# A preact-conv pair on one core: five written-out programs, a shorter first-unit program for GpSimd, and the last residual in the sums

## What is computed

```python
    def _L1_conv_ref(x, w1, w3, w5, wd, wf):
        ...
        x1 = _conv(x, w1, padding=[(0, 0), (0, 0)])
        x2 = _conv(x, w3, padding=[(1, 1), (1, 1)])
        x3 = _conv(x, w5, padding=[(2, 2), (2, 2)])
        x4 = _conv(x, wd, padding=[(2, 2), (2, 2)], dilation=(2, 2))
        out = jnp.concatenate([x1, x2, x3, x4], axis=1)
        return _conv(out, wf, padding=[(0, 0), (0, 0)])
    ...
    x = x + _L0_conv_ref(_gn(x), ...)
    x = x + _L1_conv_ref(_gn(x), w1, w3, w5, wd, wf)
```

## Time and profile before

| | us |
|---|---|
| median of 3 runs | 1725.4 (1724.74 to 1725.86) |
| the profiled execution | 1725.26 |
| its span, first to last instruction | 1723.0 |
| PE busy | 1645.8 (96% of the span) |
| DVE busy | 1492.8 (87%) |
| ACT busy | 1011.6 (59%) |
| GpSimd (POOL) busy | 637.2 (37%) |

### The profile page before, as it was taken

The page is one execution under the profiler, slowest core; times in us unless marked ns, Lnnn a source line. Parts: engine busy times, 40 slices in busy tenths (PEclk is TensorE's granted clock), DMA queues, the critical chain, the costliest instruction groups (busy, mean ns, idle before and its releaser), DMA issues.

```text
span 1723.0 us, 39391 instructions
## 1 busy us (share of the span) xinstructions
PE 1645.8 (96%) x13285; PEld 1550.5 (90%) x13285; DVE 1492.8 (87%) x1930; ACT 1011.6 (59%) x1647; POOL 637.2 (37%) x446
## 2 busy tenths in 40 slices
PE   6999989999999997999999999899999999899998
PEld 5989959999999994999999996799999999599998
DVE  6798879999788859999978886999987887799996
ACT  2866667455285657645546666655447565765541
POOL 5799962222381005232247003323227400512232
PEclk9999979999999998999999998899999999799999
DMA  7012115666502201566630220366651121055553
GB/s 190 0 42 61 45 31 126 169 165 171 148 19 57 72 19 39 149 168 177 165 99 14 73 60 1 86 164 174 168 159 46 41 69 38 1 137 132 140 146 95
DMA packets 101181, 166.05 MB, mean 96 GB/s; under 512 B 40010, under 2 KB 74411, under 8 KB 100940
## 3 DMA queue, kind: packets, MB, share of 16 engines
q1 hardware_dynamic: 77932, 138.95, 31.8%
q10 hardware_dynamic: 23168, 26.04, 4.8%
HBM read 52.20 MB, written 25.17 MB: 45 GB/s over the span
## 4 chain that ended last, share of the span: by engine, by line
PE 70%; DVE 12%; issue 11%; ACT 3%; POOL 1%; SPq 1%; DMA 1%; DVEq 1%; ACTq 0%; POOLq 0%
PE ps L924 28%; PE ps L772 12%; PE ps L793 8%; PE ps L795 7%; PE ps L794 7%; PE ps L821 3%; PE ps L855 3%; DVE region L1557 1%; DVE region L1587 1%; DVE region L1508 1%; POOL region L670 1%; PE ps L735 1%; DVE region L1605 1%; PE ps L919 1%; DMA region<-region 1%
## 5 line engine op out<-in xcount | busy, mean ns | idle before, releaser
L924 PE MATMUL ps<-region,W 128*96 128x256 f16 (+4 forms) x7156 | 796.7, 270 | 5.7 <-DMA region<-region 5.7
L924 PEld LDWEIGHTS ps<-region,W 128*96 128x96 f16 (+2 forms) x7156 | 774.9, 122 | 20.6 <-issue 14.1
L1346 DVE TENSOR_TENSOR region<-V,band 128x2322 f32<-128x2322 f32 (+2 forms) x104 | 257.7, 2488 | 59.2 <-PE ps L795 56.1
L1122 ACT ACTIVATE region<-region 96x1584 f16<-96x1584 f32 (+1 forms) x80 | 98.1, 1273 | 311.0 <-DVE region L1519 306.2
L680 POOL TENSOR_TENSOR region<-region 96x528 f32<-96x528 f32 (+1 forms) x72 | 96.4, 1344 | 407.8 <-DVE region L1557 405.8
L793 PE MATMUL ps<-region 128*128 (+1 forms) x1152 | 228.2, 280 | 10.0 <-DVE region L1355 4.4
L795 PE MATMUL ps<-region 128*128 (+1 forms) x1152 | 222.8, 275 | 0.0
L794 PE MATMUL ps<-region 128*128 (+1 forms) x1152 | 222.3, 275 | 0.0
L1587 DVE SCALAR_TENSOR_TENSOR region<-ps,small,region 96x768 f32<-96x768 f32 (+1 forms) x220 | 203.7, 988 | 10.3 <-PE ps L924 8.5
L772 PE MATMUL ps<-proj,region 96*128 96x240 f32 x1024 | 210.1, 368 | 0.5 <-DVE region L1605 0.4
L772 PEld LDWEIGHTS ps<-proj,region 96*128 96x128 f32 x1024 | 195.2, 191 | 14.4 <-issue 1.2
(11 more groups left out here) (208 smaller groups left out, 2229.6 us busy)
## 6 DMA issues: line engine op xcount, KB each, us to landing
region<-region SPq DMA_DIRECT2D x116, 247.5 KB, 4.0
region<-in_x_dram SPq DMA_DIRECT2D x128, 192.0 KB, 2.4
out_dram<-region SPq DMA_DIRECT2D x40, 576.0 KB, 4.2
region<-region ACTq DMA_DIRECT2D x72, 247.5 KB, 2.4
X<-in_x_dram SPq DMA_DIRECT2D x30, 576.0 KB, 5.9
region<-region SPq DMA_DIRECT2D x36, 247.4 KB, 4.9
X<-in_x_dram SPq DMA_DIRECT2D x19, 384.0 KB, 11.1
region<-region SPq DMA_DIRECT2D x24, 185.6 KB, 3.8
```

Of the source, the lines that this page charges most:

```text
L924: last = mm(o, w, src, start=k == 0, stop=k == len(steps) - 1, skip_group_check=split and ck > 0)
L1346: v.tensor_tensor(T[:, i, 3 * c:3 * c + m].rearrange("p m (i j) -> p m i j", j=3), taps.broadcast_to([P, m, BW // 3, 3]), mask.broadcast_t ...
```

## The change

1. The loops over the images in SP's, GpSimd's and ACT's programs become Python loops: the four images are written out, semaphore values are constants, and the branches on `b` go.
2. GpSimd's `first_planes` ends after the differences and part 0 of blocks 1 to 4. Part 1's points and its column sums, for all five blocks, move to DVE (`second_part_edge`, `second_part`), in between the low parts of part 0 and those of part 1. They are now made by two multiply-adds and one addition.
3. The mean is put back by ACT (one activation with bias `MG2`, twice the mean, for which DVE has a new tiny step) instead of DVE.
4. ACT's order in the first unit: the copies of part 0 go ahead of part 1's high parts.
5. Last unit: DVE adds `X` to two of the three kinds of sums in `acc`, ahead of `middle_outputs`; GpSimd's `residual` for it goes, and SP's write waits for DVE.

```diff
@@ first_planes (GpSimd)
-                    twice = f32at(Y2F_AT + YF * RW, 5 * RW).rearrange("p (k e) -> p k e", k=5)
+                    twice = f32at(Y2F_AT + YF * RW, 4 * RW).rearrange("p (k e) -> p k e", k=4)
-                    def point_0_and_inf(k, end, n):
-                        done(n)
-                        take(twice[:, k:end], plane(k, end, 1), plane(k, end, 0))
-                        take(plane(k, end, 2), plane(k, end, 2), plane(k, end, 1))
-                        done(n + 2)
-                        take(plane(k, end, 0), twice[:, k:end], plane(k, end, 0))
-                        take(plane(k, end, 2), plane(k, end, 2), plane(k, end, 1))
-                        done(n + 4)
...
                     for c in range(2):
                         take(slots(0, 3, c), taps(2, c, 3), taps(0, c, 3))
-                    point_0_and_inf(1, 5, 13)
-                    column_sums(1, 5, 0, 3)
-                    pool.wait_ge(s_pl0, b * NPL0 + 1 + START)
-                    own = yb.rearrange("p r e -> p (r e)")
-                    take(pln[:, 0, 0:3 * RW], own[:, 2 * RW:], own[:, 0:3 * RW])
-                    point_0_and_inf(0, 1, 19)
-                    column_sums(0, 1, 0, 3)
...
-                for u in range(UNITS - 3, UNITS):
-                    residual(u, LASTR if u == UNITS - 1 else UR)
+                for u in range(UNITS - 3, UNITS - 1):
+                    residual(u, UR)
@@ ACT
+                one = buffers(0)[2][:, 1:5, 4 * RW:5 * RW].rearrange("p k (c j) -> p k c j", c=2)[:, :, :, 1:1 + HC]
+                act.wait_ge(s_fp, b * NFP + 10 + START)
+                act.wait_ge(s_st, sv + N_MEAN2 + 2 + START)
+                act.activation(one, one, ACT.Identity, bias=col(MG2)).then_inc(s_fix, 1)
                 deviation(N_PPRE + b * NPST + 7, 7, 1)
...
-                        act.wait_ge(s_fp, b * NFP + 23 + START)
+                        copied(0, 2)
+                        act.wait_ge(s_pl0, b * NPL0 + 8 + START)
                         plain(hi, 1)
-                        copied(0, 2)
-                        act.wait_ge(s_fp, b * NFP + 24 + START)
+                        act.wait_ge(s_pl0, b * NPL0 + 9 + START)
                         sums(hi, 1)
@@ DVE
+                def second_part_edge():
+
+                    own = yb.rearrange("p r e -> p (r e)")
+                    v.tensor_tensor(plane0(0, 0, 3), own[:, 2 * RW:], own[:, 0:3 * RW], ALU.subtract).then_inc(s_pl0, 1)
+
+                def second_part():
+
+                    slot = lambda k: pln0[:, :, k * RW:(k + 1) * RW]
+                    first_done(6)
+                    dve.wait_ge(s_fp, b * NFP + 13 + START)
+                    v.scalar_tensor_tensor(slot(0), slot(0), -2.0, slot(1), ALU.mult, ALU.add).then_inc(s_pl0, 1)
+                    v.scalar_tensor_tensor(slot(2), slot(1), -2.0, slot(2), ALU.mult, ALU.add).then_inc(s_pl0, 1)
+                    first_done(8)
+                    pairs = pln0[:, :, 0:3 * RW].rearrange("p k (q e) -> p k q e", e=RW)
+                    v.tensor_tensor(cs0[1].rearrange("p k (q j) -> p k q j", j=PC), pairs[:, :, :, PC:RW],
+                                    pairs[:, :, :, 1:1 + PC], ALU.add).then_inc(s_pl0, 1)
...
-                for part in range(2):
-                    lows(0, 0, 0, 0, part)
+                second_part_edge()
+                lows(0, 0, 0, 0, 0)
+                second_part()
+                lows(0, 0, 0, 0, 1)
...
                 first_rows(UNITS - 1, 2, LASTB)
+                dve.wait_ge(s_acc, (b * UNITS + UNITS - 1) * NACC + 5 + START)
+                rows = X[:, (UNITS - 1) * UR * W:].rearrange("p (r j c) -> p c r j", j=HC, c=2)
+                for r in range(OR):
+                    n = len(range(r, LASTR, OR))
+                    kinds = acc[:, r, 1:3, 0:n * HC].rearrange("p c (k j) -> p c k j", j=HC)
+                    v.tensor_tensor(kinds, kinds, rows[:, :, r:LASTR:OR], ALU.add).then_inc(s_pre, 1)
+                dve.wait_ge(s_pre, (b + 1) * OR + START)
                 middle_outputs(UNITS - 1, LASTB)
```

61 lines of the change are left out of this document (31 added, 30 removed).

## The result

The changed kernel takes **1711.99 us** (median of 4 runs, 1711.63 to 1713.19) against 1725.12 us for the kernel before, measured beside it (1724.74 to 1725.86). The ratio is 0.9925, 95% interval 0.9907 to 0.9942: faster by 13.1 us, 10 to 16. The forecast was 1717.2 with a range of 1711.5 to 1725.5; the time lies in the range, near its lower end.

The account below looks back on a forecast made before the run. The prediction held each image to hang on when unit 1's low parts are placed. First unit 6.5 plus last unit 1.7 gave 8.2 us off 1725.26, 1717.1; adjusted for the median it predicted 1717.2, range 1711.5 to 1725.5.

Parts of the forecast that it names:

- GpSimd stops earlier, 4.1 us per image: x1's statistics on DVE: tiny steps no longer held by GpSimd, variance 4.1 us earlier, 3.4 in the second image.
- The mean on ACT, 0: First unit: ACT's activation of about 0.75 us is hidden before the root is wanted, so it costs nothing.
- Part 1 on DVE takes back 2.3 us: First unit, counted from S (end of L1488): L1511 starts at S+11.3, was S+8.97, losing 2.3 us per image.
- I count nothing for them: The first unit's last low DMAs, which must land ahead of L1557: issued 1.1 or 1.7 us earlier, priced at zero.
- One for one through unit 1's low parts: Every microsecond by which DVE reaches the end of L1557 earlier is a microsecond of the image.
- Net of the first unit 6.5 us: First unit over four images: 1.8 us gained in each of three images and 1.1 in the second.
- The last unit 1.7 us, and nothing between images: DVE's additions replace GpSimd's residual: 1.7 us gained at the program's end, nothing between images.
- Loops written out, "I count zero": ACT's 2.60 us stop at the loop's return: removal worth zero; on the path, three would give 7.8 us.
- This rival: PE's clock drops in the longer wait at unit 1: 2.6 us an image, 1727.6 if all fall; chance 0.12.
- The rival that the hold isn't GpSimd's: DVE's tiny steps stay at 1.24 us, so nothing is gained at the variance: 1732.9; chance 0.05.
- That of new code on SP or ACT: Fetching new code in each image stops SP or ACT; four stops like ACT's 2.60 us give 1727.6; chance 0.05.
- That unit 1 is no longer bound by its low parts: DMAs land faster or DVE's work is shorter, so all of the earlier start counts: 1708.0; chance 0.08.

Follow-up runs that it names:

- hold_read: Changed kernel with four more GpSimd subtractions of 528 elements, each waiting for the one before, behind the two differences: 1714.67 us.
- hold_set: Changed kernel with nine GpSimd memsets of 528 elements, which read nothing, behind the two differences: 1711.96 us.
- hold_long: Changed kernel with six GpSimd subtractions of 528 elements, back to back, behind the two differences: 1720.75 us.
- before: The kernel before, without any of the edits, measured beside the others: 1725.12 us beside the changed kernel.
- a_loops: Kernel before with only the loops over the images written out on SP, GpSimd and ACT: 1722.53 us, ratio 0.9991.
- c_last: Kernel before with only the last unit's edit (x added on DVE ahead of the middle outputs): 1722.97 us, ratio 0.9993.
- points_first: Changed kernel with both of part 1's multiply-adds on DVE moved ahead of part 0's low parts: 1707.68 us.
- delay_low: Changed kernel with four more DVE steps of 0.31 us each between the planes and low parts of unit 1: 1717.09 us.
- points_split: Changed kernel with only the first of part 1's two multiply-adds moved ahead of part 0's low parts: 1710.68 us.
- b_first: Kernel before with only the first unit's edit (mean on ACT, part 1's points and sums on DVE), loops kept: 1714.37 us, ratio 0.9943.

## Why the prediction was right in sign, and 5 us short

**GpSimd stops earlier, 4.1 us per image: right.** The two profiled executions give 4.28, 3.46, 4.29 and 4.30 (forecast 4.1, 3.4, 4.1, 4.1), 16.3 against 15.7. That it is GpSimd's subtractions, and not GpSimd being busy, is shown by `hold_read`, `hold_set` and `hold_long`. One reading was loose: the prediction has all three tiny steps end with an operation of 528 elements, but L1479 ends with the sum of 792 behind them (1500.70), which is why it is the longest. The short second image was a matter of that one execution: eleven of the twelve images of `before`, `a_loops` and `c_last` have 7.1 to 7.2 us from the `MEAN2` matmul to the variance, only this one 6.4. With the usual value the term is 17.0. The Trainium skill, SBUF — State Buffer, section "SBUF: two separate sides", has a VectorE operation with two SBUF inputs take part in the lock only against a GpSimd operation that reads SBUF. The runs agree: nine memsets held nothing, and the one-input L1484 was not held.

**The mean on ACT, 0: right.** It takes 0.72 us and ends 0.6 us before the root's input is there.

**Part 1 on DVE takes back 2.3 us: right in kind, too large by a fifth.** From the variance matmul to unit 1's first plane step it was 10.18 us in the fourth image and is 12.03, so 1.85. The new pieces were priced a little low (0.84, 0.83 and 1.19 us where 0.78, 0.78 and 1.1 stood), ACT's high parts rightly (1.95). The error lies ahead of them: counted from S (now 1491.31), part 0's low parts begin at 1.48 us and not 1.66, take 2.40 and not 2.49 for their first two pieces, and the points are ready at S+5.4 in place of S+5.8. From there on my chain holds to 0.05 us (L1516 at S+10.9 for S+11.3). But "I count nothing for them", said of the first unit's last low DMAs, was wrong in one image. In the fourth, SP's last one (L376) is issued 14.0 us behind the variance matmul and lands at 19.4, where it was 12.1 and 16.7, and DVE stands for it:

```profile
1509.82 4.49 DVE L1562 TENSOR_TENSOR region<-region 96x1584 f16<-96x1584 f32 x4 [0.54 <-DMA region<-region]
```

So at the end of unit 1's low parts this image has lost 2.33 us, the forecast figure, but by luck: a term that was too large and one that was missing. The second image waits 0.44 us (0.47 before), the other two don't wait for it now. In the mean over the images this point moved by 1.9 us. Over the four images 8.4 us were given back, against 9.2.

**One for one through unit 1's low parts: shown in the mean of four images, not image by image.** Earlier by 1.4 us per image gave 1.4 (`points_first`), later by 0.8 cost 0.7 (`delay_low`, in which the lower clock also acted); earlier by 0.4 gave 0.75 (`points_split`), about one for one within the noise of 0.3 us an image. But the reason is a little other than I wrote. I had only the landing in mind. Where it lands early, as in images 1 and 3, PE then runs up against DVE's own period; that DVE's chain passes a delay on in full by this way is not shown (image 1 of `delay_low` grew by 0.2 us for 1.0).

**Net of the first unit 6.5 us: measured 7.9.** 0.6 of the difference is the tiny steps, 0.8 part 1. The sum is nearer than its terms: mean to next fell by 1.2, 1.4, 2.9 and 2.4 us in the four images, where 1.8, 1.1, 1.8 and 1.8 were forecast. The prediction saw that PE did not wait at unit 1 in the third image and kept its 1.8; it didn't wait there in the first image either, which the prediction missed, and just these two came out furthest below and above.

**The last unit 1.7 us, and nothing between images: right.** 1.8 us behind the last matmul. DVE's three additions take 1.36 us where 1.4 was said.

**Loops written out, "I count zero": wrong by about 1 us.** I looked only at ACT's stop of 2.60 us and found it covered. I didn't follow the output's DMA, for which DVE waits before the last unit's rows and PE's projection behind them, though the earlier trace rows had that wait in it. `a_loops` also has 0.5 us less around the span, for which the prediction had no term. The Trainium skill, Runtime: NRT & Kernel Launch, section "Instruction fetch mechanics", has a taken branch wait for a fetch when its target lies outside the two pages at hand. No run shows what ACT's stop was made of; it went with the loop, but the 7.8 us that three stops would have given didn't come.

**The rest, some 2 us, is in no step.** 0.5 lies around the span. Most of the other part is the first projection, which took 53.26 us in the profiled execution of the kernel before and 52.01 in that of the changed one. Windows of the kernel before and then of the changed one:

```profile
48.00:50.00 2.00, 2.00 (x8) 1.72 (x7) 0.00 (x0) 0.48 (x1) 0.00 (x0) 1.00 0.00 0
```

```profile
48.00:50.00 2.00, 2.00 (x12) 1.88 (x11) 0.55 (x1) 1.47 (x4) 0.00 (x0) 1.00 0.00 0
```

In the kernel before each of the first six matmuls (from 47.00 on) takes 0.40 us and each later one 0.20, and eight take 2.87 us where they take 1.62 in the changed kernel: that is the whole 1.25 us. The window shows a clock of 1.00, but the trace's first entry of a granted clock stands at 49.5 us, just where the matmuls become fast, and time without an entry is printed as 1.00. The doubled length speaks for the lower level of the clock up to there. The other traces agree: where the first entry comes 2.2 and 2.0 us into the projection (`points_first`, `hold_long`) it takes 53.1 and 53.0 us, and where it comes within 0.1 us of its start or before it, 52.0 to 52.1. Up to this point the kernels do the same work, so it belongs to executions and not to the edit. Added up, the edits are worth 7.9 + 1.2 + 1.8 = 10.9 us, the first image's start and what lies around the span make 2.1 in these two executions, and the medians differ by 13.1.

**The rivals.** In the changed kernel the clock stayed at 1.00 through both waits before unit 1. Windows of the changed kernel (the third number from the end is the granted clock):

```profile
1515.00:1519.00 4.00, 2.63 (x23) 2.25 (x21) 4.00 (x6) 2.17 (x3) 2.03 (x2) 1.00 0.94 222
1519.00:1523.00 4.00, 2.85 (x24) 2.60 (x24) 3.97 (x5) 0.00 (x0) 0.00 (x0) 1.00 0.60 121
1523.00:1525.00 2.00, 0.98 (x9) 0.98 (x10) 1.90 (x3) 1.72 (x2) 0.00 (x0) 1.00 0.01 1
```

This rival was nearer than that execution shows. Behind the same wait the granted clock fell to its lower level for about 3.4 us in the fourth image of `b_first` (PE had stood 1.84 us) and of `hold_set` (1.82), the very wait that it came through at 1.00 in the changed kernel (1.84), and in all four images of `delay_low`. The 24 matmuls then took 4.5 us for 2.8. The 1.7 us hardly showed in the time, since L904 would have waited about as long for its DMA (1.69 us in the changed kernel): in `hold_set` it starts 33.8 us behind the variance matmul as in the changed kernel. So the mechanism was right and is not excluded, but the price of 2.6 us an image was too high here.

The rival that the hold isn't GpSimd's fell. That of new code on SP or ACT left no stop in the stretches read, and `a_loops` was not slower. That unit 1 is no longer bound by its low parts fell too, in the changed kernel; in `points_first` it is nearly true.

## What to carry to other kernels

Look for DVE steps whose time has nothing to do with their size: a step on one number that takes 1.2 us stands behind a GpSimd operation with inputs, here a subtraction or a sum, and the cure is to move that GpSimd work, even onto DVE itself. Then follow the engine that gained up to the next place where another waits for it, and look at both waits there: where DVE and ACT wait for each other in turn, one exchange in the order of DVE's steps was worth about 4 us, a third of the whole change. And when a trace is the basis of a sum, look at more than one image of it: a single lucky one (3.4 in place of 4.2 us) and a single slow start (1.3 us in the first projection) were both in the one execution that I had.

## What the runs showed of the hardware

GpSimd memsets of 528 elements, nine in 5.27 us, leave DVE's two-input steps on one number at 0.15 to 0.21 us; subtractions of the same size stretch them to between 0.3 and 1.2 us, up to the end of a GpSimd instruction. A one-input step of 0.15 us beside such a subtraction is not stretched. Where the subtractions wait for each other, a DVE step can start in the 0.08 us between two of them and go through (L1486, 0.15 us, between two that were held), but it doesn't always (L1479, 1.9 us). Four in a chain made the variance 0.9 us later, six without a gap 1.6 to 2.5 us.

Behind a wait of PE of 1.7 to 1.8 us at unit 1 the granted clock held in one execution and fell to the lower level for 3.4 us in others of nearly the same kernel.

The last of the low parts' DMAs of unit 1 (L364, behind six others on SP's queue) lands 2.0 to 2.2 us after its issue in images 1 and 3 of the changed kernel and 3.3 to 3.5 in images 2 and 4.
